# Where the double lookups begin: pair 0 looked up alone, and the pairing of the cycles shifted by one

## The reference

```python
e = stack([tbl_f[ids[:, f]] for f in range(27)], axis=1)      # 2048 x 27 x 128
z = einsum('bnd,bmd->bnm', e, e)[:, i, j]                     # i < j: 351 products a sample
h = concatenate([z, dense_ctx], axis=1)                       # 351 + 16
h = maximum(h @ W_top1 + b_top1, 0)                           # 367 -> 512
h = maximum(h @ W_top2 + b_top2, 0)                           # 512 -> 256
y = h @ W_top3                                                # 256 -> 1
```

## Time and profile before

| | |
|---|---|
| median of 3 runs | 361.74 us (361.22 to 362.67) |
| the profiled execution, its own time | 363.08 us |
| its span, first to last instruction | 361.3 us |
| mean granted TensorE clock | 0.988 |
| PE busy | 338.1 us (94%) |
| VectorE, ScalarE, GpSimd busy | 222.8, 178.1, 243.0 us (62, 49, 67%) |
| DMA | 44.05 MB, mean 122 GB/s |

### The profile page before, as it was taken

How to read it: one execution, slowest core, us unless ns; L and a number is a source line. 1 busy time by engine, 2 the same in 40 slices (tenths; PEclk the granted TensorE clock), 3 DMA queues, 4 the chain that set the end, 5 groups by cost and what they waited for, 6 DMA issues and landing times.

```text
span 361.3 us, 8195 instructions
## 1 busy us (share of the span) xinstructions
PE 338.1 (94%) x3478; PEld 284.3 (79%) x3478; DVE 222.8 (62%) x160; ACT 178.1 (49%) x303; POOL 243.0 (67%) x263
## 2 busy tenths in 40 slices
PE   4999999999999999999999999999999999998860
PEld 1666779887888889888888888888888889987760
DVE  4999995899229942899049922999149903602011
ACT  4655885543644373534654364334473465553310
POOL 6777777777777777777777777777777777750000
PEclk9999999999999999999999999999999999999986
DMA  6956795864247934844247725775276625741300
GB/s 176 231 142 168 176 271 121 186 174 119 53 53 182 165 103 49 188 148 145 54 79 177 187 62 45 193 146 146 54 121 141 114 54 86 176 90 30 51 21 0
DMA packets 54122, 44.05 MB, mean 122 GB/s; under 512 B 39953, under 2 KB 44125, under 8 KB 54087
## 3 DMA queue, kind: packets, MB, share of 16 engines
q1 hardware_dynamic: 44135, 26.52, 33.8%
q0 software_dynamic: 8192, 16.79, 19.9%
q10 hardware_dynamic: 1760, 0.22, 0.4%
HBM read 36.43 MB, written 7.09 MB: 120 GB/s over the span
## 4 chain that ended last, share of the span: by engine, by line
PE 80%; ACT 5%; DMA 4%; issue 4%; DVE 3%; SPq 1%; ACTq 0%; DVEq 0%
PE emb_ps L537 21%; PE emb_ps L539 20%; PE gram_ps L565 12%; PE mlp_ps L582 11%; PE mlp_ps L591 8%; PE emb_ps L548 6%; DMA gram<-tbl_rows 3%; DVE table_lo L694 2%; ACT emb L774 1%; DMA last_products<-gram 1%; DVE onehot L678 1%; ACT h L800 1%; ACT gram L785 1%; DMA z<-last_products 1%; ACT emb L755 1%
## 5 line engine op out<-in xcount | busy, mean ns | idle before, releaser
L511 POOL DMA_INDIRECT rows<-tbl_rows,idx x256 | 242.2, 946 | 78.8 <-issue 73.5
L678 DVE TENSOR_TENSOR onehot<-ids_b,row_id 125x2048 fp32r<-125x2048 int32 x72 | 158.9, 2279 | 33.3 <-PE emb_ps L539 29.1
L537 PE MATMUL emb_ps<-onehot,table_hi 125*128 125x512 f32 (+1 forms) x400 | 148.2, 380 | 3.7 <-DVE table_lo L694 2.2
L539 PE MATMUL emb_ps<-onehot,table_lo 125*128 125x512 f32 (+1 forms) x400 | 143.3, 368 | 0.0
L537 PEld LDWEIGHTS emb_ps<-onehot,table_hi 125*128 125x128 f32 x400 | 76.3, 191 | 21.6 <-DVE table_lo L694 3.8
L539 PEld LDWEIGHTS emb_ps<-onehot,table_lo 125*128 125x128 f32 x400 | 76.4, 191 | 10.8
L706 DVE TENSOR_TENSOR mlp_ps<-mlp_ps,rows 128x256 f32<-128x256 f32 x16 | 6.9, 432 | 91.8 <-PE mlp_ps L591 91.8
L565 PEld LDWEIGHTS gram_ps<-emb 128*54 128x54 f32 x2048 | 53.4, 130 | 6.5 <-issue 3.0
L565 PE MATMUL gram_ps<-emb 128*54 128x54 f32 x2048 | 56.1, 214 | 2.2 <-ACT emb L755 0.8
L754 ACT COPY held<-emb_ps 128x256 f32<-128x256 f32 x38 | 14.2, 373 | 82.8 <-PE emb_ps L539 82.8
L785 ACT COPY gram<-gram_ps 118x432 f32<-118x432 f32 x64 | 33.1, 518 | 41.2 <-PE gram_ps L565 34.8
(11 more groups left out here) (23 smaller groups left out, 73.9 us busy)
## 6 DMA issues: line engine op xcount, KB each, us to landing
ids_b<-ids_onehot SPq DMA_DIRECT2D x33, 256.0 KB, 6.4
products<-gram SPq DMA_DIRECT2D x28, 216.0 KB
gram<-tbl_rows SPq DMA_DIRECT2D x9, 480.0 KB
rows<-tbl_rows,idx POOLq DMA_INDIRECT x256
z<-products SPq DMA_DIRECT2D x14, 126.0 KB
h<-tbl_rows SPq DMA_DIRECT2D x2, 480.0 KB
z<-products SPq DMA_DIRECT2D x7, 112.0 KB
w_sb<-w SPq DMA_DIRECT2D x1, 768.0 KB, 6.7
```

Source lines behind the costliest of these rows:

```text
L511: pool.indirect_dma_start(out=rows[:, t, f, :], out_offset=None, in_=gathered_tables[f], in_offset=bass.IndirectOffsetOnAxis(ap=idx[:, p, ...
L537: nc.tensor.matmul(ps[:, 0:width], table_hi[0:ROWS, k, j, :], columns[:, c, :], start=j == 0, stop=False)
L539: last = nc.tensor.matmul(ps[:, 0:width], table_lo[0:ROWS, k, j, :], columns[:, c, :], start=False, stop=j == ROWS_PER - 1)
L678: nc.vector.tensor_tensor(onehot[0:ROWS, seq % ONEHOT_RING, :].rearrange("p (j b) -> p j b", b=width), *operands, ALU.is_equal).then_inc(o ...
```

## The change

Only the list is changed. Pair 0 looks up both sets by single lookups. The doubles begin with pairs 1 and 2 for the set of five, and with pairs 2 and 3 for the set of six (pair 1 looks the set of six up alone). At the end pair 7 has the set of five alone.

```diff
-LOOKUPS = [(0, 0, 2), (1, 0, 1), (1, 1, 2), (0, 2, 2), (1, 3, 2), (0, 4, 2), (1, 5, 2), (0, 6, 2), (1, 7, 1)]
+LOOKUPS = [(0, 0, 1), (1, 0, 1), (0, 1, 2), (1, 1, 1), (1, 2, 2), (0, 3, 2), (1, 4, 2), (0, 5, 2), (1, 6, 2), (0, 7, 1)]
```

## The result

The changed kernel took 371.54 us, median of 4 runs (369.14 to 373.5), against 361.72 us (361.22 to 362.67) for the kernel before on the same chip: a ratio of 1.0253, interval 1.0221 to 1.0286. It is slower, by more than three times what was forecast (364.4), and lies outside the range of 362.2 to 367.6. The profiled execution took 373.5 us with a span of 371.7, so the trace has 10.4 us more than the one before.

The account below looks back on a forecast made before the run. VectorE was taken to bound the first cycle, PE the loop. Terms -9.3 + 0.5 + 9.2 + 0.3 + 4.0 - 2.0 = +2.7 us took the profiled 363.08 to 365.8, 1.3 above the median: forecast 364.4 us, range 362.2 to 367.6.

Parts of the forecast that it names:

- cost the gathers at nothing: GpSimd's gathers: PE reaches pair 2 and later 0.7 to 5 us later, so none is late; cost 0.
- (a): First cycle: five pieces leave VectorE, -11.0 us, less 1.7 lost at the start; -9.3 us.
- (b): Table loads in the first cycle: they fit VectorE's pace, with a late start; +0.5 us, far bound +3.5.
- S: The start of cycle 1, forecast at about 55.4 us in place of 64.19.
- the 1.7 allowed: Start of the first cycle: VectorE, free since 12.6, waits for PE's spread ids until 14.3; +1.7 us.
- (c): Cycle 1's lookups: 33.5 us where they took 24.26; +9.2 us, 1.8 of it PE waiting for VectorE.
- (d): Pair 0's product round trip in cycle 1: z stands just before PE wants it; +0.3 us.
- the ring: Three one-hot pieces made ahead, hiding VectorE's slower pace from PE for ten or twelve pieces a cycle.
- (e): Cycles 2 to 6: three of set 1 and two of set 0 instead of the reverse; +4.0 us.
- (f): Cycle 7: one single lookup less, without a turn before it; -2.0 us.
- The clock: Rival: PE's pauses in the first cycle lower its clock; +2.5 us, 366.9 us; chance 0.02.
- The 68% for slower: Whole kernel: chance 0.68 of measuring slower, against 0.29 same and 0.03 faster.

Follow-up runs that it names:

- spread version: Changed kernel with each of seven loads (five ids, two weights) given its own point of the program; 367.46 us, ratio 1.0135; once more: 368.41 us.
- half pieces: Spread version with VectorE making only the first half of each one-hot piece of cycle 1; 365.7 us, ratio 1.0073.
- changed kernel, first / again: The changed kernel as first measured, 371.54 us, ratio 1.0253, and repeated without further edit, 373.47 us, ratio 1.0301.
- ids late: Changed kernel with cycle 1's five loads of ids held back until pair 0's eight banks are turned; 375.02 us, ratio 1.0294.
- weights late: Changed kernel with the two weight loads held back until pair 0's eight banks are turned; 372.92 us, ratio 1.0241.
- both late: Changed kernel with ids, then weights, held back until pair 0's eight banks are turned; 378.6 us, ratio 1.0375.
- pair 0 alone: Against the kernel before: set of five looked up singly for pairs 0 and 1, everything from cycle 2 on unchanged; 371.05 us, ratio 1.0196.
- both late, padded: Both late with 24 more small matmuls ahead of pair 0's gram products; 377.67 us, one run.

## Why the prediction was wrong, and where it was right

**The step that failed** is the one that cost the gathers at nothing: "PE comes to pair 2 and later 0.7 to 5 us later than before, so no gather is late". The comparison began with pair 2. For pair 0, where PE was to come 9 us *earlier* while GpSimd's pace of 1.25 us stayed, it was not made. The rows for it were there: 32 gathers of 1.25 us from about 3 us put the last issue at 41.6, and the forecast's own last `turn` stood at about 45. That left 3 to 4 us for a landing whose length no row quoted, while the change itself moved nine loads from 41 us to 34 and the forecast had no term for them. The pace alone would have passed: where the burst is not in the way the landing takes 2.5 to 3.1 us (six executions). What was left out is the landing under the burst, and the trace of the kernel before had it, 7.3 us. Measured: a landing of 8.57 us, a wait of 4.2, and 2.0 behind it at the lower clock. The spread version, which differs only in where the seven loads stand, gets these 6.2 us back in the trace.

**(a) and (b), first cycle: right but 1.4 us short.** Without the late gather S is 56.82 (spread version), forecast 55.4, before 64.19. The steps of 3.39 us were right. The start lost more than the 1.7 allowed: 1.62 us before 14.34 as forecast, and then three more gaps of 0.5 us (17.14, 18.92 above, and 29.74) while PE and ScalarE caught up, against 0.5 in all in (b).

**(c) and (d): right.** +9.53 against +9.5 with z never waited for, 13 pieces in a row behind the ring, and the half pieces show the split between VectorE's share (2.1) and PE's (7.4). What the first cycle sheds, the second pays. Two slips in the working change no time: by the earlier trace rows piece k starts at S + 2.2 + 2.20 (k - 4), and the last load of ids waits for piece 11, not 10; the times used, S + 22.1 and S + 19.9, are those of the right pieces.

**(e): right**, +4.04 against +4.0, and shown by its absence in the version that keeps the old pairing from cycle 2 on. **(f): 0.3 us short.** `place_held` moves six features' halves there now and ScalarE needs 3.0 us for it instead of 2.5, which holds the first bank.

**The rival "The clock" was given 0.02 and is real, though small.** The forecast reckoned with pauses of 0.4 to 0.8 us. They are longer, because a late table or a late copy holds PE. Of ten profiled executions with a first cycle of single lookups, six had it fall between 19 and 35 us:

| profiled execution | longest idle of PE, 14 to 30 us | lowest granted clock in 5 us, 20 to 35 us | last split starts |
|---|---|---|---|
| half pieces | 0.30 | 1.00 | 44.98 |
| changed kernel, first / again | 1.05 / 2.02 | 1.00 / 1.00 | 45.52 / 45.43 |
| spread, first / again | 1.17 / 2.11 | 1.00 / 0.50 | 45.62 / 46.58 |
| ids late | 1.22 | 0.65 | 46.97 |
| weights late | 1.46 | 0.50 | 48.77 |
| both late | 1.53 | 0.61 | 47.51 |
| pair 0 alone | 1.62 | 0.74 | 46.97 |
| both late, padded | 1.64 | 0.68 | 46.67 |

Where it falls the last split starts 1.1 to 3.3 us later than in the changed kernel (in the 3.3 a table that took 6.62 us to land has a share). Three profiled executions with the old list have no idle of PE there and a clock of 1.00. In the changed kernel such a fall costs nothing more, since the late gather ends the cycle anyway; without the burst it does, and it is a likely part of the spread version's scatter of 366.3 to 370.1 us. So is the tail, where the clock stayed up behind the wait for z in five of the thirteen profiled executions. Why a gap of 2.02 us left the clock up and one of 1.22 did not stays open. The Trainium skill, "TensorE: Matmul & The Clock Gate", "Why this matters for your kernels", warns of gaps between bursts: here gaps of 1.22 us and more were followed by a fall in six executions, where the forecast had felt safe because none would be longer than a third of the 2.60 us in the earlier trace rows.

So of the 7.7 us that the prediction missed in the trace, 6.2 were the burst on the last gather, 1.4 the start of the first cycle, and 0.3 cycle 7, less 0.3 in the tail. The 68% for slower were right in sign, and not by the burst's help: the spread version is 1.35% slower too, where 0.7% was forecast. The range was too narrow, because none of its cases was about pair 0's gathers.

**What stays open**: by what the burst delays a gather. It is not a matter of the ids alone. In the kernel before the weights' 6 KB packets ran from 43.24 to 48.26 and the first of the ids' at 47.70, and the gather issued at 41.60 had landed at 48.90. Nor is it in proportion to the bytes of the ids: with loads of half the size the gather still took 8.14 us. The Trainium skill, "DMA: Bandwidth & Descriptors", "Queues, rings and completion order", has each DMA engine alternate between queue rows packet by packet. In the changed kernel the engines started 214 packets of ids and 9 of the gathers' 4 KB ones between 44 and 47 us, so either these were not turn for turn or the gathers' packets were not ready. No run here tells which.

## What to carry to other kernels

When a change makes a stage shorter, list every stream that does *not* get shorter with it (here gathers at 1.25 us each) and compare its end with the stage's new end, in the first cycle too. Then look at what the earlier end triggers: a queue that is through its work sooner starts its next burst sooner, onto whatever is then in flight. Of the placements of the burst tried on the changed kernel, only the one spread over the program left PE waiting neither for a gather nor for instructions in the first cycle.

Where two engines are nearly level, work taken from one cycle and given to the next is paid for there: in the spread version five pieces off the first cycle gave 7.4 us, and the second, with four pieces and five lookups more, cost 10.2.

## What the runs showed of the hardware

- A gather of 128 rows of 512 bytes landed 2.5 to 3.1 us after its issue in six executions without the burst around it, and 8.1 to 8.7 us in four in which five broadcast loads of ids had been issued from 36.3 to 40.8 us, just ahead of it. In the kernel before, with loads of weights behind it, it took 7.3 us.
- PE can stop for want of instructions: 4.13 to 6.00 us with the DMA engines' share at 0.82 to 1.01, always at the same place of its program, and moved by exactly the 24 matmuls that were put ahead of it. Each time a 16 KB packet of the queue of kind "instruction" had landed 1.3 to 1.4 us before PE went on. Stops of up to 1.67 us came at shares of 0.12 to 0.26 too.
- A wait of 4.2 us left PE at the lower level (0.52 over the next 6.3 us), a stop of 6.0 us at 0.50 behind it; a gap of 1.2 to 2.1 us did so in some executions and not in others.
